# Two-layer gated attention and experts: negated maxima placed on chip, and layer 1's bounds in three buffers

## The reference

```
x = x + tanh(g_xattn[0]) * L0_attention(layernorm(x), ctx)   # 16 heads of 16
x = x + tanh(g_ffn[0])   * L0_experts(layernorm(x))          # sigmoid router, 4 of 8 experts, and a shared one
x = x + tanh(g_xattn[1]) * L1_attention(layernorm(x), ctx)   # scores clipped at +-10000, a NaN anywhere -> uniform
x = x + tanh(g_ffn[1])   * L1_experts(layernorm(x))          # softmax over the top 2 of 8 experts
```

## Time and profile before

| what | value |
| --- | --- |
| three runs | 1070.68 us median (1070.47 to 1071.9) |
| the profiled execution | 1065.39 us, of it 1063.6 us from the first to the last instruction (the span) |
| PE / DVE / ACT / POOL busy | 87% / 71% / 46% / 22% of the span |
| mean granted TensorE clock | 0.896 of full speed |
| DMA queue of SP | 128.11 MB, 48.5% of 16 engines' span |

### The profile page before, as it was taken

How to read it: one execution, slowest core, us unless ns; L and a number is a source line. 1 busy time by engine, 2 the same in 40 slices (tenths; PEclk the granted TensorE clock), 3 DMA queues, 4 the chain that set the end, 5 groups by cost and what they waited for, 6 DMA issues and landing times.

```text
span 1063.6 us, 17907 instructions
## 1 busy us (share of the span) xinstructions
PE 922.6 (87%) x6385; PEld 736.5 (69%) x6385; DVE 754.2 (71%) x1489; ACT 486.1 (46%) x842; POOL 235.0 (22%) x386
## 2 busy tenths in 40 slices
PE   3568999999999999898897676785489999999995
PEld 2345677777777676676665444553389999999995
DVE  3634667777667678788867578963768888888882
ACT  2125644444444444334343333442256676667762
POOL 2011211020210000201010122421135444454423
PEclk9557999999999999899998766865589999999998
DMA  6996746056055116365462874341366776677742
GB/s 151 265 176 140 132 78 109 23 95 103 31 84 84 31 55 123 94 120 107 128 124 91 161 150 111 93 131 40 110 239 209 233 233 220 202 227 236 230 140 30
DMA packets 121080, 142.03 MB, mean 134 GB/s; under 512 B 11456, under 2 KB 105304, under 8 KB 120864
## 3 DMA queue, kind: packets, MB, share of 16 engines
q1 hardware_dynamic: 110512, 128.11, 48.5%
q0 software_dynamic: 8832, 12.25, 5.3%
q10 hardware_dynamic: 1648, 0.53, 0.2%
HBM read 109.97 MB, written 30.88 MB: 132 GB/s over the span
## 4 chain that ended last, share of the span: by engine, by line
PE 62%; DVE 14%; DMA 10%; SPq 4%; issue 4%; ACT 3%; POOL 2%; ACTq 0%; POOLq 0%; DVEq 0%
PE bank L947 12%; PE bank L786 8%; PE by_key L931 6%; PE by_query L931 6%; PE bank L796 5%; PE value_bank L730 4%; DVE rowmax L1267 3%; PE by_query L693 3%; PE by_key L712 3%; DMA max<-shiftT 3%; PE bank L640 3%; PE bank L757 3%; PE bank L679 2%; DVE probs L1292 2%; PE bank L649 2%
## 5 line engine op out<-in xcount | busy, mean ns | idle before, releaser
L1267 DVE TENSOR_REDUCE rowmax<-by_query 128x4 f32<-128x1024 f32 x128 | 155.5, 1215 | 27.2 <-PE by_query L693 27.0
L1077 ACT ACTIVATE probs<-by_key 128x1024 f32<-128x1024 f32 x128 | 130.7, 1021 | 66.6 <-PE by_key L712 63.8
L1721 POOL TENSOR_SCALAR rstd<-moments 128x2 f32<-128x2 f32 x32 | 9.6, 300 | 545.6 <-DVE moments L1231 545.6
L1772 POOL DMA_INDIRECT out_x<-x,token_i x46 | 78.2, 1700 | 146.6 <-ACT x L1182 136.6
L693 PE MATMUL by_query<-stack_k,stack_q 48*128 48x256 f32 x512 | 71.0, 359 | 38.3 <-DVE rowmax L1267 20.6
L947 PE MATMUL bank<-w_hi,h_hi 128*128 128x256 f32 x368 | 104.1, 283 | 0.0
L947 PE MATMUL bank<-w_lo,h_hi 128*128 128x256 f32 x368 | 104.1, 283 | 0.0
L947 PE MATMUL bank<-w_hi,h_lo 128*128 128x256 f32 x368 | 104.1, 283 | 0.0
L693 PEld LDWEIGHTS by_query<-stack_k,stack_q 48*128 48x128 f32 x512 | 43.6, 210 | 77.3 <-issue 46.1
L1110 ACT ACTIVATE act_gate<-bank 128x256 f32<-128x256 f32 x72 | 27.6, 383 | 142.4 <-PE bank L786 140.0
L712 PE MATMUL by_key<-stack_q,stack_k 50*128 50x256 f32 x512 | 66.8, 342 | 29.2 <-DMA stack_q<-max 26.3
(11 more groups left out here) (228 smaller groups left out, 2141.4 us busy)
## 6 DMA issues: line engine op xcount, KB each, us to landing
w<-in_L_ffn_W SPq DMA_DIRECT2D x46, 1024.0 KB, 8.7
lower<-max SPq DMA_DIRECT2D x64, 256.0 KB, 3.8
stack_k<-qk SPq DMA_DIRECT2D x96, 128.0 KB, 5.0
stack_q<-qk SPq DMA_DIRECT2D x96, 128.0 KB, 7.4
qk<-hi SPq DMA_DIRECT2D x31, 256.0 KB, 3.5
qk<-lo SPq DMA_DIRECT2D x31, 256.0 KB, 4.1
rows<-w_gate SPq DMA_DIRECT2D x8, 264.0 KB, 3.6
x<-in_x SPq DMA_DIRECT2D x8, 256.0 KB, 8.0
```

Source lines behind the costliest of these rows:

```text
L1077: ac.activation(probs[i % 4][:, :, :, :].rearrange("p k h s -> p h k s"), by_key[:, :, :].rearrange("p h (k s) -> p h k s", k=2), ACT.Exp) ...
L1267: dv.tensor_reduce(rowmax[u % 2][:, 2 * p:2 * p + 2, :], by_query[:, :, :].rearrange("p h (t s) -> p h t s", t=TT), AX, ALU.max).then_inc( ...
L1772: po.indirect_dma_start(out[:, :], bass.IndirectOffsetOnAxis(ap=token_i[:, n:n + 1].bitcast(U32), axis=0), ysb[i % 3][:, t, :], None, comp ...
```

## The change

`place_shift` issues four DMAs straight from `shiftT` to the stack rows: for each half and each part one of 16 rows of 512 B into one partition. To make the rows of one half contiguous, `rowmax` is kept by half and then by pair. Only the bounds still go to DRAM (`lower_dram`, layer 1 alone). `load_lower` uses three buffers, waits for the clip of three pairs before and for the bounds' store, reads its pair as two pieces of 1 KB, and is issued behind the slot's stages, one slot ahead of its old place; p = 0 is issued there too.

```diff
-    max_dram = [nc.dram_tensor(f"max_{l}", (NB, 3 * H * TT, P), F32).ap() for l in range(2)]
+    lower_dram = nc.dram_tensor("lower", (NB, H * TT, P), F32).ap()
-    rowmax = [sba(f"rowmax{i}", [P, H, TT]) for i in range(2)]
+    rowmax = [sba(f"rowmax{i}", [P, 2, PAIRS, TT]) for i in range(2)]
-    lower = [sba(f"lower{i}", [P, 2, S]) for i in range(2)]
+    lower = [sba(f"lower{i}", [P, 2, S]) for i in range(3)]
...
         def place_shift(u):
             l, b = layer_of(u), batch_of(u)
             sp.wait_ge(sem.shiftT_ready, u + 1)
-            rows = 3 * H * TT if l else 2 * H * TT
-            sp.dma_start(max_dram[l][b, 0:rows], shiftT[0:rows, :]).then_inc(sem.shift_out, 16)
-            sp.wait_ge(sem.shift_out, 16 * (u + 1))
-            src = max_dram[l][b, 0:2 * H * TT].rearrange("(j h two t) q -> two j h (t q)", j=2, two=2, t=TT)
             for side in range(2):
-                o = HALF * side + FULL
-                sp.dma_start(stack_q[u % SETS][o:o + 2, :, :].bitcast(F32), src[side]).then_inc(sem.shift_in, 16)
+                for part in range(2):
+                    row, src = HALF * side + FULL + part, (2 * part + side) * PAIRS * TT
+                    sp.dma_start(stack_q[u % SETS][row:row + 1, :, :].bitcast(F32).rearrange("o a (t q) -> o (a t) q", t=TT),
+                                 shiftT[src:src + PAIRS * TT, :]).then_inc(sem.shift_in, 16)
             if l:
-                load_lower(u, 0)
+                sp.dma_start(lower_dram[b], shiftT[2 * H * TT:3 * H * TT, :]).then_inc(sem.lower_out, 16)

         def load_lower(u, p):
             b = batch_of(u)
             j = PAIRS * b + p
-            if j >= 2:
-                sp.wait_ge(sem.clip_done, j - 1)
-            sp.dma_start(lower[j % 2][:, :, :].rearrange("p h s -> p (h s)"),
-                         max_dram[1][b, 2 * H * TT + 2 * p * TT:2 * H * TT + (2 * p + 2) * TT]
-                         .rearrange("r q -> (r q)").partition_broadcast(P)).then_inc(lower_in[j % 2], 16)
+            if j >= 3:
+                sp.wait_ge(sem.clip_done, j - 2)
+            sp.wait_ge(sem.lower_out, 16 * (b + 1))
+            sp.dma_start(lower[j % 3][:, :, :], lower_dram[b].rearrange("(h a t) q -> a h (t q)", h=2, t=TT)[p]
+                         .partition_broadcast(P)).then_inc(lower_in[j % 3], 16)
...
         for g in range(SLOTS_IN_ALL):
-            u, p = divmod(g - base(0) - LAG, PAIRS)
-            if NB <= u < UNITS and p < PAIRS - 1:
-                load_lower(u, p + 1)
             for stage, n in PLAN[2 * g - 3] + PLAN[2 * g - 2]:
                 if stage in stages:
                     stages[stage](n)
+            u, p = divmod(g + 1 - base(0) - LAG, PAIRS)
+            if NB <= u < UNITS:
+                load_lower(u, p)
...
         def scores_by_key(u, p):
             if p == 0:
-                pe.wait_ge(sem.shift_in, 32 * (u + 1))
+                pe.wait_ge(sem.shift_in, 64 * (u + 1))
...
         def shift_turn(u):
             if u:
-                ac.wait_ge(sem.shift_out, 16 * u)
+                ac.wait_ge(sem.shift_in, 64 * u)
+            if u > NB:
+                ac.wait_ge(sem.lower_out, 16 * (u - NB))
```

More of the change, by code:

```diff
@@ L163 @@
 k_mm k_hi k_lo q_mm q_hi q_lo x_plus obias_mm obias_ready mean_mm mean_ready k_out q_out k_in0 k_in1 k_in2 q_in0 q_in1 q_in2 v_mm v_ready
-qk1_done max_done shift_chain shift_ready shift_turned shiftT_ready shift_out shift_in
-lower_in0 lower_in1 qk2_done clip_done exp_done pv_done taken values_turned recip_done normal_done attn_turned
+qk1_done max_done shift_chain shift_ready shift_turned shiftT_ready lower_out shift_in
+lower_in0 lower_in1 lower_in2 qk2_done clip_done exp_done pv_done taken values_turned recip_done normal_done attn_turned
 attnT_ready wo_done x0_ready z_ready z_out
@@ L354, in build @@
     ctx_in, ctxT_in = (sem.ctx_in0, sem.ctx_in1), (sem.ctxT_in0, sem.ctxT_in1, sem.ctxT_in2)
-    lower_in = (sem.lower_in0, sem.lower_in1)
+    lower_in = (sem.lower_in0, sem.lower_in1, sem.lower_in2)
     z_in = (sem.z_in0, sem.z_in1, sem.z_in2, sem.z_in3)
@@ L1266, in maxima @@
             dv.wait_ge(sem.qk1_done, i + 1)
-            dv.tensor_reduce(rowmax[u % 2][:, 2 * p:2 * p + 2, :], by_query[:, :, :].rearrange("p h (t s) -> p h t s", t=TT),
+            dv.tensor_reduce(rowmax[u % 2][:, :, p, :], by_query[:, :, :].rearrange("p h (t s) -> p h t s", t=TT),
                              AX, ALU.max).then_inc(sem.max_done, 1)
         def shifts(u):
-            flat = rowmax[u % 2][:, :, :].rearrange("p h t -> p (h t)")
+            flat = rowmax[u % 2][:, :, :, :].rearrange("p h a t -> p (h a t)")
             dv.wait_ge(sem.max_done, PAIRS * (u + 1))
@@ L1288, in clip @@
             prob = probs[i % 4][:, :, :, :].rearrange("p k h s -> p k (h s)")
-            dv.wait_ge(lower_in[j % 2], 16 * (j // 2 + 1))
+            dv.wait_ge(lower_in[j % 3], 16 * (j // 3 + 1))
             dv.wait_ge(sem.exp_done, i + 1)
-            bound = lower[j % 2][:, :, :].rearrange("p h s -> p (h s)").unsqueeze(1).broadcast_to([P, 2, 2 * S])
+            bound = lower[j % 3][:, :, :].rearrange("p h s -> p (h s)").unsqueeze(1).broadcast_to([P, 2, 2 * S])
             dv.scalar_tensor_tensor(prob, prob, 1.0, bound, ALU.min, ALU.max).then_inc(sem.clip_done, 1)
```

## The result

The changed kernel took 1040.38 us (median of four runs, 1036.33 to 1049.79), the kernel before 1070.58 beside it (1066.05 to 1071.9). The ratio is 0.9743, interval 0.9701 to 0.9784; it is worked out from the single runs and is not the quotient of the medians. The forecast was 1036.0, likeliest range 1027 to 1047, whole range 1022 to 1058. The profiled execution took 1040.59 us, of it 1038.8 span; before, 1065.39 and 1063.6.

What follows compares the result with a forecast made beforehand. PE paces layer 1, DVE close behind, stalled by late maxima. 20.9 (stalls) + 10.2 (bounds) + 7.5 (clock) - 3.5 (given back) = 35 us: 1030.4 profiled, 1036 on the runs' scale, range 1027 to 1047, whole 1022 to 1058.

Steps and rivals of the forecast that it cites:

- SP when it is held, and the stalls: Layer 1: SP issues the maxima's placement in time, so the seven by-key stalls of units 9 to 15, 25.1 us, go.
- Direct placement: Maxima go straight to the stack rows without DRAM: arrival 4.4 us after the ACT copy, between 2.7 and 7.5.
- rule against it: Argument against four placements: at about 2.0 us fixed for each small transfer, one after another, an estimated 8 us.
- Units 9 to 12: Layer 1: their stalls counted at 11.8 us, as PE paces there and DVE idles with it.
- the clock's term: Layer 1: without stalls, PE's work behind them runs at the upper clock: 2.9 + 1.7 + 2.9 = 7.5 us.
- The give-back: Units 9 to 12: DVE is late next, PE loses time to other waits as in unit 8, some 3.5 us.
- Bounds and stacks: Layer 1: bounds asked for earlier end DVE's two waits, stack transfers move with them: 6.1 + 4.1 = 10.2 us.
- units 13 and 15 I count at DVE's idle time: Layer 1: these two units' by-key stalls counted only as far as DVE idles, 4.50 and 3.44 us.
- DVE did not take over: Rival, chance 0.20: DVE takes the stall's place in layer 1, only its idle time comes back: about 17 us, 1054.
- More comes back: Rival, chance 0.08: all stalls, bounds, stacks, clock and half of another low-clock stretch come back: 50 us, 1021.
- serial placements: Rival, chance 0.04: the four go one behind another, arrival 12.6 us after the copy, some 10 us gained: 1061.
- a slow write: Rival, chance 0.06: writing into one partition is slow; kernel slower from arrival at 10.2 us, 1128 at 14.

Runs made afterwards that it cites:

- e1: Kernel before with the maxima placed straight on chip, two bounds' buffers and the load in its old places: 1061.84 us, ratio 0.9936.
- e4: Changed kernel, three buffers kept, with the bounds' load back in its old places at the slot's head: 1044.73 us, ratio 0.9771.
- e2: Kernel before with three bounds' buffers and the load at the slot's tail, maxima still through DRAM: 1042.97 us, ratio 0.9763.
- e12: The changed kernel itself, run and profiled again, against the kernel before: 1040.52 us, ratio 0.9741.
- e6: Changed kernel with the bounds written in pair order, one 2 KB piece per partition: 1038.22 us, ratio 0.9737, against 1038.92 for the changed kernel beside it.
- e8: The changed kernel itself, run and profiled again, against the kernel before: 1038.92 us, ratio 0.9738.
- The fillers: Changed kernel with throwaway products in PE's idle times from unit 15 on: 1037.02 and 1038.38 us; with bounds also in pair order 1036.80.
- e5: Kernel before with PE running throwaway by-key products in the stalls of units 9 to 15: 1069.06 us, ratio 1.0026.

## Why the prediction was right, and where its sum was off

*SP when it is held, and the stalls.* Right: placements 0.03 to 1.03 us after the copy in units 9 to 15, and PE waits at no first by-key scores. e1 to e4 show that the release, one clip earlier, does it.

*Direct placement.* The arrival was taken as 4.4 us after the copy; measured 5.3 in unit 9, 5.5 in unit 15 and 5.0 to 6.1 in units 9 to 15, inside the bounds of 2.7 to 7.5. In unit 9 the four issues took 2.40 us, as estimated, and the last landed 2.8 us behind them in place of 2; in unit 15 it was 3.47 and 1.5. The room of 9.9 and 5.9 covered it, in unit 15 with 0.28 us left. The old way took 6.4 from SP's arrival to PE's start, so the leg that is gone was worth about 1 us of arrival (0.6 in e1), and that behind a room that hides it. The prediction gave the two causes one sum and didn't say that the second could do without the first: e2 would have been the same forecast. The estimated 8 us of its rule against it did not happen: unit 9 took 5.2 us from the first issue to the last landing. The Trainium skill (DMA: Bandwidth & Descriptors, Anatomy of one DMA) gives the 2.0 us for each transfer on GpSimd's path, and doesn't say that they are paid one after another; these transfers were issued by SP, and here they overlapped.

*Units 9 to 12.* From unit 8's first by-key scores to unit 12's the time fell by 12.3 us, where 12.9 was predicted. PE's idle time (length less busy time) and its busy time tell the terms apart. The rows of units 9 and 11 before, to be set beside those of the changed kernel above:

```profile
430.66:481.87 51.21, 48.09 (x282) 34.90 (x282) 40.45 (x91) 19.47 (x37) 5.91 (x16) 0.91 0.49 103
...
527.12:573.95 46.83, 40.82 (x258) 29.37 (x259) 37.21 (x65) 16.82 (x31) 3.20 (x8) 0.95 0.49 115
```

PE's idle time in units 8 to 11 went from 18.7 us to 10.0 in all three profiles: 8.7 less, where 11.8 of stalls less 3.5 given back make 8.3. Its busy time, 172.3 before, was 167.7, 167.7 and 170.9: 4.6, 4.6 and 1.4 less, where the clock was to give 2.9 + 1.7 = 4.6. The 2.9 came in unit 9 in every profile (48.09 to 45.2). The 1.7 came in unit 11 in two (40.82 to 39.23 at a clock of 1.00) and not in e12's, where the clock of that unit was 0.93, PE was busy 42.46 us and the unit took 47.5 us in place of 44.2. So the clock's term did come through here, where no rows come late behind it, and it differs from one execution to the next.

The give-back was right in size, some 3.0 us (11.8 less 8.7), and of the kind that was said: PE's waits for DVE's maxima in 365 to 760 us rose from 6.1 to 13.5 (11.0 and 10.7 in the other two profiles). Its recorded working does not give it, though: 2.6 less about 1, in four units, is 6.4 and not 3.5. That the 3.5 fits is luck.

*Bounds and stacks.* The stretch from unit 12 to unit 14 gave 17.7 where 17.6 were predicted. That is closer than its terms: PE's 6.44 us for stack transfers are gone, as said, but DVE's waits for bounds went from 10.6 us to 4.9 (7.1 and 4.6 in the other two profiles) and not to nothing, and the landing, taken as 3.8, is 5.1, because two pieces of 1 KB are not as quick as one of 2 KB. In e6, with 3.6 again, no difference in time is seen.

*Where the missing 7 us are* (28.3 measured, 35.1 predicted, in spans; by the ratio of runs the gain is 27.5, 23 to 32): the forecast's time lies near the measured one, and its gain is too large. Unit 0's stall is gone, but its 1.2 can't be seen in a start that differs by 3.6 us between profiles of one kernel. Unit 15's stall, 4.23 us on PE, counted at 3.44, gave 1.0 in the mean (from 1.2 longer to 2.2 shorter), and the stretch behind it became 0.9 to 4.9 longer. Taken together, the time from unit 14's first by-key scores to the token table was 108.9 before and 115.0, 109.1 and 107.9 after: nothing was won there. This is the step that was wrong, "units 13 and 15 I count at DVE's idle time": unit 13's term came out in its stretch, unit 15's did not. Behind unit 15 each batch of layer 1's input is finished in a chain, seen in the chain of waits of the changed kernel:

```profile
662.22 0.76 DVE stats L1227 x2
663.41 1.03 POOL rstd L1721
...
668.68 0.59 ACT w_gate L1041
669.41 1.08 PE bank L668 x4
```

From DVE's statistics (662.22) to PE's turn (669.41) it is 7.2 us, 4.7 of it eight small POOL instructions one after another, and PE waits for such chains: 9.8 us, 3 times, in this profile and in e8, whose stretches are 76.8 and 74.4, and 7.4 in e12, whose stretch is 72.8. Before it was 7.0, twice, in a stretch of 71.9, with PE standing 4.23 for the maxima just ahead of it. So it looks as if the time won ahead of this chain is waited for in it. That the old stall hid part of the chain is argued from these waits; no run took the chain out, and the cause stays open. The fillers raise the clock of the last stretch from 0.55 to 0.85 and don't settle it either.

The rivals: DVE did not take over (busy 37.14 of 44.75 us in unit 8, 41.14 of 45.94 in unit 9; 1054 is above every run of the changed kernel), though PE waits for it more than before. "More comes back" (1021) is refuted by the time, serial placements and a slow write by arrivals of 5.0 to 6.1 us.

## What to carry to other kernels

When an in-order DMA queue stands at a wait for a buffer, look at what is queued behind it: the buffer's own data may have time while the transfer behind it has none, and one more buffer frees both. Before a transfer is made shorter, compare its arrival with the moment the reader needs it under the order that you will have: here the shorter way was worth 0.6% alone, and once the queue was free some 0.2%, inside the noise. Before a stall at the end of a stage is counted, look at the serial chain behind it: here a stall of 4.2 us went and the end of the stage came no earlier. And when a filler is to test the clock, read the granted clock behind every stall that it was meant for before the result is read.

## What the runs showed of the hardware

- A broadcast of 256 KB from DRAM to 128 partitions landed in 3.5 to 3.8 us with one 2-KB piece per partition and in 4.9 to 5.8 with two of 1 KB (medians of five and of nine profiles). The Trainium skill (DMA: Bandwidth & Descriptors, Why small descriptors are slow) holds joining of pieces to be worth it at 256 B or less, and its figure of three cycles per packet of 32-byte beats would make two pieces of 1 KB an estimated 4 to 5% slower than one of 2 KB. That figure is for the packets alone; the measured difference, from issue to landing, is some 40%.
- Four DMAs of 16 rows into one partition cost SP 0.59 us apiece and land 2.2 us after their issue, both in the median (landing 1.7 to 5.4), so that they overlap:

```profile
L520 SPq DMA_DIRECT2D stack_q<-shiftT x64: 503/589/1676, 66.8 to 661.4; - x64
...
DMA to landing us min/median/max: 1.7/2.2/5.4
```

- Filler in a stall raised the granted clock behind it from 0.50 to 1.00 in unit 9 and left it at 0.65 and 0.50 in units 11 and 12 (e5). The time moved by +0.26% (-0.03 to +0.56).
- In the changed kernel, where no rows come late, a unit's length goes with the clock: unit 11 took 44.2 us at a mean granted clock of 1.00 (two profiles) and 47.5 at 0.93 (e12), and PE was busy 39.2 and 42.5 us of it.
